# Matmul weights of an attention and feed-forward kernel loaded by GpSimd's converting transfers instead of SyncE's plain ones

## What is computed

```python
x = x + xattn(layernorm(x), ctx, ctx, ctx)      # gelu(x ctx^T) * (x ctx^T), times ctx, 120 context rows per batch
x = x + ffn(layernorm(x), w1, w2, h1, h2, w3, ...)
# ffn, with _tlin(x, w, s) = (x @ w.T) * s, all weights float32 and ternary (-1, 0, 1)
h = silu(_tlin(x, w1_w, w1_s)) * _tlin(x, w2_w, w2_s)      # 256 -> 1024
h = gelu(_tlin(h, h1_w, h1_s))                             # 1024 -> 1024
h = gelu(_tlin(h, h2_w, h2_s))                             # 1024 -> 1024
return _tlin(h, w3_w, w3_s)                                # 1024 -> 256
```

## Time and profile before

| what | value |
|---|---|
| median of 3 runs | 340.53 us (340.48 to 341.97) |
| the profiled execution's own time | 340.34 us |
| its span, first to last instruction | 338.6 us |
| instructions | 4807 |
| TensorE (PE) busy | 329.3 us, 97% of the span |
| VectorE (DVE) busy | 256.3 us, 76% |
| ScalarE (ACT) busy | 207.2 us, 61% |
| GpSimd (POOL) busy | 19.4 us, 6% |
| DMA | 68.61 MB, mean 203 GB/s |
| granted TensorE clock | 0.999 |

### The profile page before, as it was taken

How to read it: one execution, slowest core, us unless ns; L and a number is a source line. 1 busy time by engine, 2 the same in 40 slices (tenths; PEclk the granted TensorE clock), 3 DMA queues, 4 the chain that set the end, 5 groups by cost and what they waited for, 6 DMA issues and landing times.

```text
span 338.6 us, 4807 instructions
## 1 busy us (share of the span) xinstructions
PE 329.3 (97%) x1668; PEld 278.9 (82%) x1668; DVE 256.3 (76%) x476; ACT 207.2 (61%) x338; POOL 19.4 (6%) x44
## 2 busy tenths in 40 slices
PE   7799999999999999999999999999999999999994
PEld 5589888888888888888899888888888888888894
DVE  3577889649969697897776544697888698977784
ACT  2755725394843465777794235468686778577940
POOL 4121023002202000000000000000000000000000
PEclk9999999999999999999999999999999999999999
DMA  6799999699939758344430640036556634333003
GB/s 236 253 360 409 394 397 400 241 354 375 317 126 347 269 190 310 128 136 178 175 135 0 201 174 0 2 133 239 189 186 204 243 128 171 124 127 124 0 15 119
DMA packets 22541, 68.61 MB, mean 203 GB/s; under 512 B 1632, under 2 KB 3040, under 8 KB 18784
## 3 DMA queue, kind: packets, MB, share of 16 engines
q1 hardware_dynamic: 22512, 68.25, 55.9%
HBM read 57.75 MB, written 18.87 MB: 226 GB/s over the span
## 4 chain that ended last, share of the span: by engine, by line
PE 96%; DVE 2%; issue 1%; POOL 0%; ACT 0%; POOLq 0%; DVEq 0%
PE P L1285 45%; PE P L1348 17%; PE P L1238 17%; PE P L1374 9%; PE P L1202 2%; PE P L1186 2%; PE P L1194 2%; PE P L1384 1%; PE P L1437 0%; PE P L1423 0%; DVE xs L851 0%; DVE xn L839 0%; DVE st L832 0%; PE P L1430 0%; ACT xt L570 0%
## 5 line engine op out<-in xcount | busy, mean ns | idle before, releaser
L1285 PE MATMUL P<-TR,WR 128*128 128x512 f32 x672 | 152.6, 389 | 0.0
L1285 PEld LDWEIGHTS P<-TR,WR 128*128 128x128 f32 x672 | 126.1, 188 | 26.2
L924 DVE TENSOR_TENSOR TR<-H,TR 128x512 fp32r<-128x512 f32 x84 | 57.5, 689 | 18.5 <-ACT TR L623 16.4
L623 ACT ACTIVATE TR<-H 128x512 fp32r<-128x512 f32 x84 | 52.5, 629 | 20.9 <-DVE H L919 15.7
L1238 PE MATMUL P<-X,W 128*128 128x512 f32 (+1 forms) x320 | 61.4, 349 | 0.1
L1348 PE MATMUL P<-TR,WR 128*128 128x512 f32 x256 | 61.4, 395 | 0.0
L1238 PEld LDWEIGHTS P<-X,W 128*128 128x128 f32 x320 | 51.7, 189 | 8.1 <-DVE X L857 0.5
L1348 PEld LDWEIGHTS P<-TR,WR 128*128 128x128 f32 x256 | 47.7, 188 | 9.7
L613 ACT ACTIVATE SL<-P,sc 128x512 f32<-128x512 f32 (+1 forms) x40 | 24.0, 604 | 34.1 <-PE P L1238 33.4
L897 DVE SCALAR_TENSOR_TENSOR H<-P,sc,SL 128x512 f32<-128x512 f32 (+1 forms) x40 | 25.4, 640 | 23.9 <-PE P L1238 16.0
L664 ACT ACTIVATE H<-H,sc 128x512 f32<-128x512 f32 x36 | 26.0, 721 | 16.0 <-DVE H L940 15.9
(11 more groups left out here) (67 smaller groups left out, 209.9 us busy)
## 6 DMA issues: line engine op xcount, KB each, us to landing
WR<-blocks_h SPq DMA_DIRECT2D x27, 1024.0 KB, 4.9
H<-in_h SPq DMA_DIRECT2D x8, 1024.0 KB, 11.3
blocks_h<-H SPq DMA_DIRECT2D x8, 1024.0 KB, 6.5
blocks_h<-in_h SPq DMA_DIRECT2D x7, 1024.0 KB, 13.8
stage<-in_w SPq DMA_DIRECT2D x4, 512.0 KB, 7.2
WR<-last_w SPq DMA_DIRECT2D x2, 1024.0 KB, 4.8
xs<-in_x SPq DMA_DIRECT2D x7, 256.0 KB, 11.1
out<-xs SPq DMA_DIRECT2D x6, 256.0 KB, 6.5
```

The source lines that it names most:

```text
L623: eng.activation(TR[:, f % RING, 0, :], operand(c, L, s, kk), ACT.Copy).then_inc(s_hi, 1)
L924: eng.tensor_tensor(TR[:, f % RING, 1, :], operand(c, L, s, kk), TR[:, f % RING, 0, :].bitcast(f32), ALU.subtract).then_inc(s_lo, 1)
L1285: out_ = eng.matmul(bank(c, L, s, m)[:, :], WR[r % WRING][:, at:at + 128], TR[:, f % RING, h, :], start=(s in FRESH and kk == 0 and h == 0 ...
```

## The change

GpSimd now issues the loads of `W12` and of every plain block, straight from the inputs to fp32r tiles; a transfer whose two types differ (float32 to fp32r) converts. `stage`, `copy_w`, `block_out`, `blocks` of plain weights and `last_w` are gone. Entry 1 of each `square` (block 2 plus block 3) is loaded by two transfers of GpSimd, the second of which adds to what is in the buffer, behind a wait for the first. Sums for products 2, 3 and 4 still go through the scratch and SyncE (`sums_out` writes three rows of 256 KB, not four). All 22 tests now read second loads by SyncE into `xn[0]` and `xt` and work in place there: three beside `square(0, 1)`, two beside `layer4`, eight beside `layer1(2)` and `layer1(3)`, seven beside `square(1, 0)`, two beside `square(1, 1)`, none beside `eight`.

```diff
-                eng.dma_start(dst, raw(q)).then_inc(s_S[q], 16)
+                eng.dma_start(dst, raw(q)[:, 0:3, :]).then_inc(s_S[q], 16)
...
@@ GpSimd
+            def load_w12(i):
+                eng.dma_start(W12[:, i % 2, i // 2, :], w12[i % 2][:, i // 2, :]).then_inc(s_w12[i], 16)
+            def load_block(r, w, blk):
+                if r >= WRING:
+                    reuse(eng, r - WRING)
+                eng.dma_start(place(r).rearrange("p (k o) -> p k o", k=4), w[:, :, blk, :]).then_inc(s_v[r % WRING], 16)
+            def load_both(c, L):
+                r = entry(c, L, 1)
+                w = (h1, h2)[L]
+                to = place(r).rearrange("p (k o) -> p k o", k=4)
+                reuse(eng, r - WRING)
+                eng.dma_start(to, w[:, :, 2, :]).then_inc(s_acc, 16)
+                eng.wait_ge(s_acc, 16 * (layer_no(c, L) + 1))
+                eng.dma_start(to, w[:, :, 3, :], accum_op=ALU.add).then_inc(s_v[r % WRING], 16)
...
             rstd_half(0, 0)
             rstd_half(0, 1)
+            load_w12(0)
             rstd(0, 1, 1)
+            for i in range(1, 4):
+                load_w12(i)
             rstd_half(1, 0)
             rstd_half(1, 1)
-            rstds(2, (1, 1), (0, 2), (0, 3), (1, 2), (1, 3), (0, 4), (0, 5), (1, 4), (1, 5))
-            rstds(11, (0, 6), (0, 7), (1, 6), (1, 7))
+            load_w8(0)
+            load_w8(1)
+            load_w8(2)
+            rstds(2, (1, 1), (0, 2), (0, 3))
+            load_w8(3)
+            rstds(5, (1, 2), (1, 3), (0, 4), (0, 5))
+            load_w8(4)
+            rstds(9, (1, 4), (1, 5), (0, 6), (0, 7))
+            load_w8(5)
+            load_w(0, 1, 0)
+            rstds(13, (1, 6), (1, 7))
+            load_both(0, 1)
+            load_w(0, 1, 5)
+            load_w(0, 1, 6)
+            load_w3(0)
+            load_layer(1, 0)
+            load_layer(1, 1)
+            load_w3(1)
...
@@ SyncE
             def load_check(i):
                 if i >= 2:
-                    eng.wait_ge(s_ab, ORDER.index(("again", i - 2)) + 1)
+                    eng.wait_ge(s_fl, i - 1)
...
@@ TensorE, layer1(0)
                         if i < 2:
-                            eng.wait_ge(s_cp, 3 + i)
+                            eng.wait_ge(s_w12[i], 16)
+                            eng.wait_ge(s_w12[2 + i], 16)
```

More of the change, by code:

```diff
@@ L128, in xattn_ffn @@
         s_S = [sem(f"s_S{i}") for i in range(8)]
-        s_blk = [[sem(f"s_blk{n}{i}") for i in range(4 - n)] for n in range(2)]
-        s_w3 = sem("s_w3")
+        s_acc = sem("s_acc")
         s_w = [sem(f"s_w{i}") for i in range(WRING)]
+        s_v = [sem(f"s_v{i}") for i in range(WRING)]
         s_chk = [sem("s_chk0"), sem("s_chk1")]
@@ L226, in pair_done, with summed, loads @@
                 eng.wait_ge(s_tf, EIGHT[i][1] + 4)
+        def summed(r):
+            return any(entry(c, L, s) == r for c, L in ((0, 1), (1, 0), (1, 1)) for s in STORED)
+        def loads(r):
+            return sum(summed(n) == summed(r) for n in range(r % WRING, r + 1, WRING))
         def weights_in(eng, r):
-            eng.wait_ge(s_w[r % WRING], 16 * (r // WRING + 1))
+            eng.wait_ge((s_w if summed(r) else s_v)[r % WRING], 16 * loads(r))
         GELU = {(0, 1): 0, (1, 1): 4, (0, 0): 8, (1, 0): 12}
@@ L273, in operand, with beside1, tested, reuse @@
             return tile(source(c, L), PLAIN[s] if s in PLAIN else SUMS[s][2], kk)
[L278 to L291, removed]
+        TESTS = 22
+        BESIDE = {(0, 1, 0): 0, (0, 1, 5): 1, (0, 1, 6): 2, (1, 1, 0): 20, (1, 1, 1): 21}
+        BESIDE.update({(1, 0, p): 13 + p for p in range(NP)})
+        BESIDE4 = {2: 3, 6: 4}
+        def beside1(t, m):
+            return 5 + m // 2 if t == 2 and m % 2 == 1 else 9 + m // 2 if t == 3 and m % 2 == 0 else None
+        def tested(i):
+            return (xn[0], xt)[i % 2][:, :, :, :].rearrange("p a b d -> p (a b d)")
+        def reuse(eng, r):
+            if r < 4:
+                eng.wait_ge(s_u, r + 1)
+            elif r < 6:
+                eng.wait_ge(s_tf, EIGHT[2 + r][1] + 4)
+            else:
+                c, L = max(at for at, n in ENTRIES.items() if n <= r)
+                if L < 2:
+                    eng.wait_ge(s_tf, fill(c, L, r - ENTRIES[c, L], 3) + 1)
+                else:
+                    eng.wait_ge(s_tf, FILLED[c + 1, 0])
         block = ctx.enter_context(nc.Block())
@@ L328, in load_w8 @@
[L328 to L336, removed]
-                r = entry(c, L, s)
[L338 to L344, removed]
+                dst = wS[("h1", "h2")[layer_of(q)]][:, :, q % 4, :].rearrange("s p o -> p s o")
@@ L446, in _ @@
                 eng.dma_start(out_v[b], xs[:, 2 * b:2 * b + 2, :]).then_inc(s_out, 16)
[L447 to L458, removed]
+                if q == 1:
+                    load_check(6)
+            load_sum(1, 0, 2)
+            for i in range(7, 15):
+                load_check(i)
+            load_sum(1, 0, 3)
+            load_check(15)
+            load_sum(1, 0, 4)
+            for i in range(16, TESTS):
+                load_check(i)
+            for p in STORED:
+                load_sum(1, 1, p)
             for q in range(2):
@@ L513, in _, with load_w3, load_layer @@
+            def load_w3(c):
+                r = ENTRIES[c, 2]
+                reuse(eng, r - WRING)
+                eng.dma_start(place(r).rearrange("p (k o) -> p k o", k=8), w3).then_inc(s_v[r % WRING], 16)
+            def load_layer(c, L):
+                load_w(c, L, 0)
+                load_both(c, L)
+                load_w(c, L, 5)
+                load_w(c, L, 6)
             rstd_half(0, 0)
             rstd_half(0, 1)
+            load_w12(0)
             rstd(0, 1, 1)
+            for i in range(1, 4):
+                load_w12(i)
@@ L533, in _, with magnitude @@
         def _(eng):
[L534 to L555, removed]
+            def magnitude(i):
                 eng.wait_ge(s_chk[i % 2], 16 * (i // 2 + 1))
-                magnitude(ORDER.index(("again", i)), (xn[0], xt)[i % 2][:, :, :, :].rearrange("p a b d -> p (a b d)"))
+                eng.activation(tested(i), tested(i), ACT.Abs).then_inc(s_ab, 1)
             def table(func):
                 eng.activation(spare[:, :], mhalf[:, :], func).then_inc(s_tab, 1)
-            def copy_w(i):
-                eng.wait_ge(s_w12[i], 16)
-                eng.activation(W12[:, i % 2, i // 2, :], stage[i][:, :], ACT.Copy).then_inc(s_cp, 1)
             def copy_t(b):
@@ L689, in square @@
                                 hi4(c, 1, i)
-                        if i == (3 if s == 0 else 2) and L == 1 and s in (0, 5, 6):
-                            test_h(c, s)
-                        if i == 2 and (c, L) == (1, 0):
-                            test_again(s)
-                        if i == 2 and (c, L, s) == (1, 1, 1):
-                            test_again(7)
+                        if i == (3 if s == 0 and c == 0 else 2) and (c, L, s) in BESIDE:
+                            magnitude(BESIDE[c, L, s])
             def eight(half):
@@ L747, in layer1 @@
                         hi(1, 0, 0, m // 2)
+                    if beside1(t, m) is not None:
+                        magnitude(beside1(t, m))
             table(ACT.Gelu_apprx_tanh)
@@ L778, in _ @@
                     hi4(c, 0, k)
+                    if c == 0 and k in BESIDE4:
+                        magnitude(BESIDE4[k])
                 if c == 0:
@@ L978, in square @@
                                     lo4(c, 1, i - 1)
[L979 to L986 removed]
+                    if (c, L, s) in BESIDE:
+                        test(BESIDE[c, L, s])
             def combine(q):
@@ L1028, in eight @@
                         gate(b + 1)
-                    if i < 7:
-                        test(ORDER.index(("eight", i)))
             def last(c, half, q):
@@ L1088, in layer1 @@
                         lo(1, 0, 0, m // 2 - 1)
+                    if beside1(t, m) is not None:
+                        test(beside1(t, m))
                 if t == 1:
@@ L1129, in _ @@
                         last(c, 1, k // 4)
+                    if c == 0 and k in BESIDE4:
+                        test(BESIDE4[k])
                 if c == 0:
```

105 lines of the change are left out of this document (28 added, 77 removed).

## The result

The changed kernel takes 356.5 us (356.14 to 357.61, 4 runs) against 340.5 (340.28 to 341.97, 4 runs): 1.0466 times as long, 95% interval 1.0428 to 1.0503. Its profiled execution took 356.41 us, its span is 354.5. The forecast was 343.4 us with a range to 351: the sign was right, the size was not.

A forecast was written before the change was run, and what follows sets the result against it. TensorE was taken as the bound. From the profiled 340.34 us, +1.2 for the start and +1.0 and +0.7 for `load_both` gave 343.2, against the median 343.4 us; range for 8 in 10: 340.2 to 351.

The forecast's parts named there:

- What bounds the kernel: TensorE, almost without a break from 15.14 us: work taken from others gives back almost nothing, TensorE's waits are paid in full.
- signs: First product of `layer1(0)` 1 to 1.5 us late for `W`; exactly two `WR` waits, before product 1 of `square(0, 1)` and `square(1, 1)`.
- Part 1: Four `W12` copies gone from ScalarE: 0, since TensorE waited for none of them.
- Part 2: Start on GpSimd: issue delay +1.0 us, weights landing at 16.9 us +1.2; side by side, the larger counts: +1.2, range 0 to 3.
- now they start near 6.6 us: At the start, w1 and w2 loads begin moving near 6.6 us, sharing the engines with SyncE's loads, and land at 16.9.
- Part 3: GpSimd's ring loads for `eight` and the load ahead of the last two norms: 0, the last covered by 0.9 us.
- Part 4: `load_both`: two transfers in series, 6.1 and 8.9 us, against 14.5 available; waits of 1.0 and 0.7 us, +1.7 in all.
- so I add 0.5 and 0.2: Allowance in us for traffic beside the `load_both` pairs of `square(0, 1)` and `square(1, 1)`, from engines busy 0.63 and 0.51 before.
- Part 5: The 22 tests in their new places: 0, test loads up to 0.8 us late but no wait reaching TensorE.
- Converting or adding is slow: Rival, chance 0.15: such transfers at half rate, two waits of 6.1 us and start weights 3 to 5 us late: 356.
- GpSimd held up by VectorE: Rival, chance 0.05: GpSimd's queue stands still while VectorE scales `xn`, 1.6 us more at the start: 345.0.
- All hidden: Rival, chance 0.37: start weights get two thirds of the bytes, two transfers in series fit 14.5 us: 340.5 to 342.2, say 341.

The follow-up runs named there:

- experiment 2: Changed kernel with the first test moved beside product 4 of `square(0, 1)` and the first two test loads behind product 3's load: 353.64 us, 2.9 less.
- experiment 8: Changed kernel with first tests and SyncE's two 1 MB start loads later, and product 2's load waiting until the adding transfer landed: 341.33 us.
- experiment 3: Changed kernel with the second transfer of each `load_both` overwriting instead of adding: 354.05 us, 2.5 less.
- experiments 5: Changed kernel with product 1's weights again a stored sum loaded by SyncE, `load_both` gone: 347.18 us, 9.3 less.
- experiment 6: Changed kernel with product 1's stored sum loaded by SyncE and the two 1 MB start loads behind w1 and w2: 341.45 us.
- 7: Changed kernel with the adding kept, the first tests and SyncE's two 1 MB start loads moved later: 346.58 us, 9.9 less.
- 1: Changed kernel with SyncE's two 1 MB start loads and what follows them waiting until w1 and w2 landed: 351.04 us, 5.5 less.
- experiment 4: Changed kernel with eight extra 512 KB GpSimd transfers into a spare buffer, plain, converting, adding, both, twice: 361.47 us, one execution, not compared.

## Why the prediction was right or wrong

**What bounds the kernel: right.** TensorE pays every wait in full, and nothing that left ScalarE or VectorE came back. The places were also right: TensorE waits for `W` at its first groups and for `WR` ahead of product 1 of `square(0, 1)`, and nowhere for a single block, a `turn` or a test. Two of its signs were off: the first product started 3.0 us later (18.14), not 1 to 1.5, and there was one wait for `WR`, not two.

**Part 1, the copies at 0: right.** **Part 2, the start: the term was mis-sized, 1.2 for 6.1.** Its half on GpSimd's queue erred the other way: an issue took 0.76 and later 0.55 us, not 1.2 (GpSimd's step at 10.34 was then waiting for VectorE, so nothing was lost there). The half on landing failed, in the step "now they start near 6.6 us". The byte shares were as its better bound had it, 0.52 against 0.28 MB; but the first packet came at 10.0 to 10.5 us, and the last piece landed at 20.06, not 16.9. Beside a queue that was not loaded, the first packet took 1.5 us. What part 2 left out altogether is the clock: 3.5 us of waiting brought another 2.1 us, as work went on at 1.2 GHz.

The rows of the issues, the changed kernel's timeline of GpSimd:

```profile
5.72 0.76 POOL L480 DMA_DIRECT2D W<-in_w  x1
...
7.81 1.66 POOL L480 DMA_DIRECT2D W<-in_w  x3
10.34 0.22 POOL L473 TENSOR_SCALAR rs<-mv 128x1 f32<-128x1 f32 x1 [0.87 <-DVE mv L821]
```

**Part 3, 0: right.** Three ring loads took 2.35 us of the queue together, and the last `turn` ran without a wait behind a load that waited for its buffer.

**Part 4: the price of adding was right, the price of company wrong, 1.0 for 10.0.** I had 6.1 us for the first transfer and 8.9 for the adding one. They took 5.1 to 7.3 and, outside `square(0, 1)`, 8.2 (in `square(1, 1)`, 282.33 to 290.5, beside 0.3 MB) and 9.0 (in `square(1, 0)`, beside 1.15 MB). The answer of the changed kernel for the adding line:

```profile
L504 POOL DMA_DIRECT2D WR<-in_h x3: 1204/1208/1251, 126.2 to 282.3; - x3
DMA to landing us min/median/max: 8.2/9.0/16.3
```

The step that failed is "so I add 0.5 and 0.2". Beside the first pair moved 4.0 MB, 3.7 of it beside the adding transfer; experiments 2 and 8 take it away piece by piece, and the transfer goes from 16.3 to 12.5 and 8.9 us, while experiment 3 takes only the adding away and leaves 13.4. I listed those transfers, and then priced them by the share that the engines had been busy before, when that traffic had another place in the queue and no second queue beside it. The wait of 7.5 us cost another 2.5 in clock, a term that the sum did not have in either part. In `square(1, 1)` my 0.7 was 0: the pair landed half a microsecond ahead of its product at 291.05. That is a narrow margin.

**Part 5, the tests at 0: right as ScalarE's and VectorE's work**, since experiments 5 and 6 keep their places and lose nothing that shows. But two of their loads, moved beside the pair, cost 2.9 us there (experiment 2), or 4.5 (7 against 1). The prediction counted that megabyte in part 4, too low. And the cover of the tests isn't wide: in experiment 4 test loads that took 5.6 to 6.6 us were enough to make TensorE wait 1.7 us for `TR`.

**The rivals.** "Converting or adding is slow" gave 356 us, and the kernel took 356.5. That is a coincidence of sums: its mechanism is refuted for converting by experiment 4, its two waits of 6.1 us were one of 7.5, and 4.6 of the 16.0 us were the clock, which it did not have. What holds of it is that adding alone is slower, by the 2.8 us that part 4 already had. "GpSimd held up by VectorE" is not shown: GpSimd's first issue of a piece of `W`, beside VectorE, took 0.76 us and the other three 0.55 in the mean, so at most 0.2 us of the start are in question. The Trainium skill (SBUF — State Buffer, Who interferes with whom) warns of this lock for VectorE's two-port forms; no run here isolates it, and the rows show no issue long enough for it to have mattered much. "All hidden" is what experiment 8 reaches but for 0.8 us, by order alone, and 6 with a stored sum in place of the pair.

The Trainium skill (DMA: Bandwidth & Descriptors, Anatomy of one DMA) gave 4.4 us for 1 MB; the trace has 5.1 to 5.2 for the first transfers of the pair in `square(0, 1)` and `square(1, 1)`, with 0.2 and 0.3 MB beside them. The measurement decides: the skill's price is 0.7 us low here. The Trainium skill (DMA: Bandwidth & Descriptors, Queues, rings and completion order) has an engine take turns between queues, a packet at a time; the counts 144 to 142 agree, the 128 to 73 of experiment 3 do not, or its packets are not the rows that the profile counts, which no run here shows.

**What stays open.** Why GpSimd's queue gets its first packet over 4 us after the issue behind a loaded queue, and whether that depends on the bytes or on the number of packets ahead, was not tried. Of experiment 8's last microsecond 0.4 us are lost at the start (it still waits 0.5 us for `W`, and `eight` begins at 35.39 instead of 35.03) and 0.4 in `square(0, 1)`. The one of experiment 6 was not traced to a place: its profiled execution has none of it.

## What to carry to other kernels

A transfer's time beside others is not its time alone plus a share of a mean: list what the other queues have issued at that moment, count packets one for one as a first estimate, and allow for a second queue that starts late behind a loaded one (4.5 us after its issue here, 1.5 without). Where two transfers in series have to fit between a buffer's release and its use, the order of the neighbours decides; holding back one load whose product comes 7 us later was worth 5.3 us here. And where TensorE is the bound, a wait can cost more than itself: here 3.5 us brought 2.1 more and 7.5 us 2.5 more at the lower clock.

## What was not expected of the hardware

- The adding halves the rate of a transfer that is alone, 0.41 MB in 2 us against 0.39 in 1: 512 KB took 7.8 us against 4.0 to 4.4 converting, and a packet of 2 KB 1.7 times the engine time of a plain one.
- Converting costs nothing that could be measured.
- GpSimd's first packet came some 4.5 us after issue beside a loaded queue, and 1.5 us beside an almost idle one.
- The granted clock was 0.50 when TensorE went on after its wait of 2.6 us, and rose again at about 24.5 us, 6 us later; after the wait of 7.5 us it rose at about 147 us, over 4 us into the work. Ahead of the first wait TensorE had been busy for 3.3 of 5.5 us, ahead of the second without a break.
